# The Mamba output product in high and low float32r parts, with the low parts made by GpSimd and multiplied a step later

## The reference

```python
y = ys + x * D                                   # state output and skip
y = y.reshape(b, L, D_INNER) * silu(z)           # gate, D_INNER = 512
y = y * rsqrt(mean(y * y, axis=-1) + 1e-05) * norm_w
return y @ out_w.T                               # 512 -> 256
# later: concatenate([v, h]) @ fc_w.T + fc_b     # folded into out_w by the kernel
```

## Time and profile before

| | us |
|---|---|
| median of 3 runs | 2471.05 |
| lowest, highest | 2468.98, 2473.85 |
| the profiled execution | 2475.43 |
| its span | 2473.6 |

### The profile page before, as it was taken

How to read it: one execution, slowest core, us unless ns; L and a number is a source line. 1 busy time by engine, 2 the same in 40 slices (tenths; PEclk the granted TensorE clock), 3 DMA queues, 4 the chain that set the end, 5 groups by cost and what they waited for, 6 DMA issues and landing times. The chain is left out here.

```text
span 2473.6 us, 42475 instructions
## 1 busy us (share of the span) xinstructions
PE 2144.9 (87%) x16632; PEld 1392.3 (56%) x16632; DVE 2005.4 (81%) x2384; ACT 1297.6 (52%) x2834; POOL 1015.1 (41%) x513
## 2 busy tenths in 40 slices
PE   8999967787787776666999978999999999999998
PEld 7877512231242221114777747777777777777776
DVE  4426799998989999994877757888888888888886
ACT  3337667767857764541232335555555555555552
POOL 1103789988989999980110001111111111111111
PEclk9999989998999999997999989999999999999999
DMA  7769332223121221103332224232222323333332
GB/s 236 247 193 260 92 70 36 42 51 75 20 53 19 37 42 23 20 12 97 109 96 77 77 65 79 76 78 72 69 69 73 78 76 95 93 88 86 86 78 60
DMA packets 299431, 204.44 MB, mean 83 GB/s; under 512 B 201696, under 2 KB 279008, under 8 KB 294624
## 3 DMA queue, kind: packets, MB, share of 16 engines
q1 hardware_dynamic: 286816, 151.39, 25.2%
q0 software_dynamic: 8704, 33.56, 3.7%
q10 hardware_dynamic: 3712, 16.78, 2.8%
HBM read 133.76 MB, written 67.90 MB: 82 GB/s over the span
## 5 line engine op out<-in xcount | busy, mean ns | idle before, releaser
L285 DVE TENSOR_TENSOR att_av<-att_att,att_v2ps 128x2816 f32<-128x2816 f32 (+2 forms) x288 | 776.0, 2752 | 37.8 <-PE att_bank L464 34.9
L285 POOL TENSOR_TENSOR att_av<-att_att,att_v2sb 128x1280 f32<-128x1280 f32 x256 | 744.8, 2931 | 54.4 <-PE att_bank L464 49.6
L464 PE MATMUL att_bank<-att_av,att_w 128*32 128x512 f32 x4096 | 551.8, 623 | 221.0 <-DVE att_av L285 191.8
L464 PEld LDWEIGHTS att_bank<-att_av,att_w 128*32 128x32 f32 x4096 | 135.1, 111 | 576.3 <-issue 283.9
L1681 DVE SCALAR_TENSOR_TENSOR mb_cv<-mb_bank,mb_cw,mb_cv 128x504 f32<-128x504 f32 (+2 forms) x480 | 343.2, 731 | 126.5 <-ACT mb_cv L1504 121.6
L630 ACT ACTIVATE att_ev<-att_bank 128x512 f32<-128x512 f32 x512 | 297.5, 595 | 272.0 <-PE att_bank L464 225.9
L1324 POOL TENSOR_TENSOR mb_rstd<-mb_ms,mb_neghalf 128x4 f32<-128x4 f32 x32 | 32.2, 1008 | 795.6 <-DVE mb_ms L1725 795.6
L1385 PE MATMUL mb_bank<-mb_xT_hi,dt_win_hi 128*128 128x512 f32 x576 | 242.0, 420 | 36.8 <-DVE mb_cv L1681 35.4
L1443 PE MATMUL mb_bank<-mb_wf,mb_y 128*128 128x256 f32 x1024 | 247.0, 389 | 0.9 <-DVE mb_y L1721 0.9
L1385 PE MATMUL mb_bank<-mb_xT_lo,dt_win_hi 128*128 128x512 f32 x576 | 229.2, 398 | 0.0
L1385 PE MATMUL mb_bank<-mb_xT_hi,dt_win_lo 128*128 128x512 f32 x576 | 229.1, 398 | 0.0
(11 more groups left out here) (182 smaller groups left out, 3328.3 us busy)
## 6 DMA issues: line engine op xcount, KB each, us to landing
att_xin<-in_x SPq DMA_DIRECT2D x32, 512.0 KB, 4.5
qk_t<-att_qk POOLq DMA_DIRECT2D x16, 1024.0 KB, 5.0
v<-att_vs POOLq DMA_DIRECT2D x16, 1024.0 KB, 5.5
mixed_t<-att_ev SPq DMA_DIRECT2D x1024, 8.0 KB
mb_dAb<-dA_rows SPq DMA_DIRECT2D x32, 512.0 KB, 5.9
mb_dAb<-dA_cols SPq DMA_DIRECT2D x32, 512.0 KB, 5.7
att_q<-qk_t ACTq DMA_DIRECT2D x8, 1024.0 KB, 10.8
att_kb<-qk_t ACTq DMA_DIRECT2D x64, 128.0 KB, 8.4
```

The costliest lines, as they stand in the source:

```text
L285: return eng.tensor_tensor(av[t % 2][:, :, d0:d1, :], a.unsqueeze(2).broadcast_to((P, 2, d1 - d0, N)), v2.unsqueeze(1).broadcast_to((P, 2, ...
L464: mm = pe.matmul(bank[r % NB][s * M:(s + 1) * M, :], w[i // WB % 2][:, i % WB, s, :], av[r // 2 % 2][:, i % 2, s * STRIP_D:(s + 1) * STRIP ...
```

## The change

The output product is split as the input projection is. `y` is rounded to a float32r part `y_["hi"]`, and `y_["lo"]` is what is left; `wf` becomes a pair as well. GpSimd makes both parts of y. The products with y's high part stand where `project` stood; those with its low part run a step later, between the fourth and the fifth group of the next input projection. Each output tile now has a bank of its own (`O_[t]`). `scale_out` moves behind nine of the fifteen taps, `times_g` ahead of it. The buffer `pv` is gone: the earlier result is loaded into the output buffer `ot` and added in place.

```diff
--- before.py
+++ after.py
@@ -1126,6 +1126,7 @@
         PR_ = bank[0:3]
         G_ = bank[3]
         YA_, YB_ = bank[4:6], bank[6:8]
+        O_ = bank[4:8]
         PAIR = SEQS // 2
         NT = TOK // P
         GR = CT + 1
@@ -1138,12 +1139,11 @@
         neghalf = sb("neghalf", [P, TT])
         win_hi, win_lo = carried.win_hi, carried.win_lo
         raw, dtt, step_of_dt, dtb, nega = carried.raw, carried.dt, carried.step, carried.dtb, carried.nega
-        wf = [sb(f"wf{d}", [P, CT, E]) for d in range(2)]
+        wf = [{n: sb(f"wf{d}_{n}", [P, CT, E], F32R) for n in ("hi", "lo")} for d in range(2)]
         cw, cb = [[sb(f"{n}{d}", shape) for d in range(2)] for n, shape in (("cw", [P, GR, TAPS]), ("cb", [P, GR]))]
         dskip, normw = [[sb(f"{n}{d}", [P, CT]) for d in range(2)] for n in ("dskip", "normw")]
         bias = sb("bias", [P, E])
         xin = [sb(f"xin{u}", [P, TT, E]) for u in range(2)]
-        pv = [sb(f"pv{u}", [P, TT, E]) for u in range(2)]
         ot = [sb(f"ot{u}", [P, TT, E]) for u in range(2)]
         xT_hi, xT_lo = sb("xT_hi", [P, KT, CHUNK], F32R), sb("xT_lo", [P, KT, CHUNK], F32R)
         cv = sb("cv", [P, GR, CHUNK])
@@ -1154,6 +1154,7 @@
         dAb = sb("dAb", [P, PAIR, NH * L])
         inj = sb("inj", [P, PAIR, NH, L])
         S = sb("S", [P, PAIR, NH * L])
+        y_ = {n: sb(f"y_{n}", [P, CT, CHUNK], F32R) for n in ("hi", "lo")}
         y = sb("y", [P, CT, CHUNK])
         ssr = sb("ssr", [P, CHUNK])
         ms, rstd = sb("ms", [P, TT]), sb("rstd", [P, TT])
@@ -1182,6 +1183,7 @@
         xtok_done, xtok_copied, g_done = sem("xtok_done"), sem("xtok_copied"), sem("g_done")
         inj_ready, scanned, s_ready = sem("inj_ready"), sem("scanned"), sem("s_ready")
         y_done, y_read, gated, squared = sem("y_done"), sem("y_read"), sem("gated"), sem("squared")
+        wf_hi_ready, y_hi_ready, y_lo_ready = sem("wf_hi_ready"), sem("y_hi_ready"), sem("y_lo_ready")
         ss_done, ss_copied, col_done, col_read, rstd_ready = (sem("ss_done"), sem("ss_copied"), sem("col_done"),
                                                               sem("col_read"), sem("rstd_ready"))
         out_done, out_read = sem("out_done"), sem("out_read")
@@ -1236,8 +1238,8 @@
                     if c == NCHUNK:
                         for u in range(2):
                             sp.wait_ge(o_stored[u], NCHUNK // 2 * 16)
-                    sp.wait_ge(out_read, TT * (c - 1))
-                    move("p", c, pv[c % 2], False, pv_loaded[c % 2])
+                    sp.wait_ge(o_stored[c % 2], io_value(c - 2))
+                    move("p", c, ot[c % 2], False, pv_loaded[c % 2])
 
             def load_decay(c):
                 if c < ALL:
@@ -1323,13 +1325,29 @@
                 need(pool, out_read, TT * c)
                 pool.tensor_tensor(rstd[:, :], ms[:, :], neghalf[:, :], ALU.pow).then_inc(rstd_ready, 1)
 
+            def y_hi(c, half):
+                need(pool, out_done, TT * c)
+                pool.wait_ge(gated, 2 * c + half + 1)
+                s = slice(2 * half, 2 * half + 2)
+                pool.tensor_copy(y_["hi"][:, s, :], y[:, s, :]).then_inc(y_hi_ready, 1)
+
+            def y_lo(c, half):
+                pool.wait_ge(y_hi_ready, 2 * c + half + 1)
+                s = slice(2 * half, 2 * half + 2)
+                pool.tensor_tensor(y_["lo"][:, s, :], y[:, s, :], y_["hi"][:, s, :], ALU.subtract).then_inc(y_lo_ready, 1)
+
             inject(0)
             pool.wait_ge(scanned, PAIR)
             inject(1)
             for k in range(ALL):
+                y_hi(k, 0)
+                y_hi(k, 1)
+                if k + 1 < ALL:
+                    pool.wait_ge(scanned, PAIR * (k + 2))
+                y_lo(k, 0)
+                y_lo(k, 1)
                 root(k)
                 if k + 2 < ALL:
-                    pool.wait_ge(scanned, PAIR * (k + 2))
                     inject(k + 2)
 
         @block.tensor
@@ -1434,15 +1452,23 @@
                                                    start=True, stop=True)
                         mm.then_inc(y_done, 1)
 
-            def project(c, t):
-                for m in range(CT):
-                    if t == 0 and m == 0:
-                        pe.wait_ge(y_read, 4 * c + 2)
-                    if t == 0 and m % 2 == 0:
-                        pe.wait_ge(gated, 2 * c + m // 2 + 1)
-                    mm = pe.matmul(YA_[t // 2][:, (t % 2) * E:(t % 2 + 1) * E], y[:, m, t * P:(t + 1) * P],
-                                   wf[way(c)][:, m, :], start=(m == 0), stop=(m == CT - 1))
-                if t % 2:
+            def project_hi(c, half, tiles):
+
+                pe.wait_ge(y_hi_ready, 2 * c + half + 1)
+                for t in tiles:
+                    if half == 0 and t % 2 == 0:
+                        pe.wait_ge(y_read, 4 * c + t + 2)
+                    for m in (2 * half, 2 * half + 1):
+                        for wn in ("hi", "lo"):
+                            pe.matmul(O_[t][:, 0:E], y_["hi"][:, m, t * P:(t + 1) * P], wf[way(c)][wn][:, m, :],
+                                      start=(m == 0 and wn == "hi"), stop=False)
+
+            def project_lo(c):
+                pe.wait_ge(y_lo_ready, 2 * c + 2)
+                for t in range(TT):
+                    for m in range(CT):
+                        mm = pe.matmul(O_[t][:, 0:E], y_["lo"][:, m, t * P:(t + 1) * P], wf[way(c)]["hi"][:, m, :],
+                                       start=False, stop=(m == CT - 1))
                     mm.then_inc(out_done, 1)
 
             def sum_squares(c):
@@ -1467,6 +1493,10 @@
                 if k >= 0 and k + 1 < ALL:
                     for i in range(NG):
                         group(k + 1, i)
+                        if i == 3 and k > 0:
+                            project_lo(k - 1)
+                if k == ALL - 1:
+                    project_lo(k - 1)
                 if k >= 0:
                     y_products(k)
                 for n, (_, _, _, first) in enumerate(PARTS):
@@ -1483,12 +1513,12 @@
                 if k == -1:
                     fold(1)
                 if k >= 0:
-                    project(k, 0)
-                    project(k, 1)
+                    project_hi(k, 0, range(TT))
+                    project_hi(k, 1, range(TT // 2))
                     sum_squares(k)
-                    project(k, 2)
+                    project_hi(k, 1, range(TT // 2, TT))
                     columns(k)
-                    project(k, 3)
+            project_lo(ALL - 1)
 
         @block.scalar
         def _(act):
@@ -1616,8 +1646,13 @@
             def scale_by_norm(d):
                 dve.wait_ge(folded, d + 1)
                 for m in range(CT):
-                    dve.tensor_scalar(wf[d][:, m, :], (YA_, YB_)[d][m // 2][:, (m % 2) * E:(m % 2 + 1) * E],
-                                      normw[d][:, m:m + 1], None, ALU.mult).then_inc(wf_ready, 1)
+                    dve.tensor_scalar(wf[d]["hi"][:, m, :], (YA_, YB_)[d][m // 2][:, (m % 2) * E:(m % 2 + 1) * E],
+                                      normw[d][:, m:m + 1], None, ALU.mult).then_inc(wf_hi_ready, 1)
+                for m in range(CT):
+                    dve.wait_ge(wf_hi_ready, CT * d + m + 1)
+                    dve.scalar_tensor_tensor(out=wf[d]["lo"][:, m, :], in0=(YA_, YB_)[d][m // 2][:, (m % 2) * E:(m % 2 + 1) * E],
+                                             scalar=normw[d][:, m:m + 1], in1=wf[d]["hi"][:, m, :],
+                                             op0=ALU.mult, op1=ALU.subtract).then_inc(wf_ready, 1)
 
             def zero_first_part():
                 for q in range(2):
@@ -1700,7 +1735,7 @@
 
             def add_skip(c, half):
                 if half == 0:
-                    need(dve, out_done, 2 * c)
+                    need(dve, y_lo_ready, 2 * c)
                     need(dve, squared, 2 * c)
                 for q in range(2):
                     dve.wait_ge(y_done, 4 * c + 2 * half + q + 1)
@@ -1731,9 +1766,9 @@
                     dve.wait_ge(rstd_ready, c + 1)
                     if c >= 2:
                         dve.wait_ge(o_stored[c % 2], io_value(c - 2))
-                dve.wait_ge(out_done, 2 * c + t // 2 + 1)
-                dve.scalar_tensor_tensor(out=ot[c % 2][:, t, :], in0=YA_[t // 2][:, (t % 2) * E:(t % 2 + 1) * E],
-                                         scalar=rstd[:, t:t + 1], in1=pv[c % 2][:, t, :] if way(c) else bias[:, :],
+                dve.wait_ge(out_done, TT * c + t + 1)
+                dve.scalar_tensor_tensor(out=ot[c % 2][:, t, :], in0=O_[t][:, 0:E],
+                                         scalar=rstd[:, t:t + 1], in1=ot[c % 2][:, t, :] if way(c) else bias[:, :],
                                          op0=ALU.mult, op1=ALU.add).then_inc(out_read, 1)
 
             zero_first_part()
@@ -1758,19 +1793,14 @@
                         for j, back in which:
                             tap(c, j, back)
 
-                taps((0, 1))
```

(16 more changed lines are left out.)

## The result

| | before | after |
|---|---|---|
| median of 4 runs, us | 2472.26 | 2453.22 |
| lowest, highest | 2468.98, 2473.85 | 2450.41, 2455.41 |
| the profiled execution | 2475.43 | 2450.41 |
| its span | 2473.6 | 2448.2 |

What follows compares the result with a forecast made beforehand. PE was taken as the bound, DVE having 3.8 us of slack in a step. 30 intervals x 1.7 = 51 us saved, less 9 around the steps, gives 42: 2471.05 - 42 = 2429 us, range 2405 to 2475.

Steps and rivals of the forecast that it cites:

- the plain step: Last stage, a step without dt work: falls from 29.89 to 28.2 us, 1.7 shorter.
- both loops: PE's work and waits, 28.2 us; and scans, low parts, low products, four groups, seed, taps, gate, scans, also 28.2.
- C: Rival, output product: short matmuls cost 0.162 us each, 2474 us in all, no change; chance 0.09.
- D: Rival, output product: weight load not hidden behind 256 columns, 0.207 us per matmul, 2540 us in all; chance 0.14.
- The price from which on the gain was to be gone: Output product: from 0.155 us per short float32r matmul, the 51 us saved shrink to the 9 lost.
- B: Rival, GpSimd's subtractions: low parts take 2.9 us each instead of 2.38, step 29.2, 2459 us in all; chance 0.16.
- the weights' scaling: Around the steps: eight more instructions scale the low output weights, four ahead of the first scans, costing 2 us.
- the end: Last step: nothing covers the low parts, and at the very end they lie beside the high products; 4 us together.
- The cast: GpSimd's rounding of y to its high part: 1.6 us for 1024 elements, the second done at 24.2, before PE asks.
- the taps' order: DVE's taps, three of the first group together: PE waits 0.2 us instead of 0.8 ahead of the fourth group.
- step (2) under "Around the steps": First twelve steps: the dt work, 5.6 us over twelve steps, loses DVE's slack, costing 3 more.
- Rival A: GpSimd's second cast holds up DVE's first scan, 0.4 us a step, step 28.6, 2441 us in all; chance 0.18.

Runs made afterwards that it cites:

- e9: The kernel before with only the changed kernel's VectorE order of taps, `times_g` and `scale_out`: 2466.82 us, ratio 0.9988 to before.
- e1: The changed kernel with the softplus pieces of dt ahead of the scans of their step on VectorE: 2435.65 us, ratio 0.9872 to before.
- e4: The changed kernel with the softplus's second instruction, a subtraction, cut to 8 columns, other columns uncorrected: 2450.54 us in a single run.
- e7: The changed kernel with each GpSimd subtraction cut in two of 512 elements, four in a step: 2448.45 us, ratio 0.9926 to before.
- e5: The changed kernel without GpSimd's subtractions, the low products reading y's high part instead: 2416.82 us, ratio 0.9798 to before.
- e3: The changed kernel with e1's edit and the low products behind the fifth projection group instead of the fourth: 2424.28 us, ratio 0.9813 to before.
- e8: e3 with `mean_square` ahead of the last scan instead of behind it: 2418.34 us, ratio 0.9787 to before.

## Why the prediction was right and wrong

**Right: the plain step.** 28.2 forecast, 28.30 measured, with both loops side by side as described. 48 matmuls cost 6.3 (24 between 2014.65 and 2017.70, eight in 1.07, sixteen in 2.16) against 6.24. Their distance is 0.12, under the 0.130 taken; what makes up for it is 0.1 to 0.2 at each change of kind. C (0.162) and D (0.207) are out. (The price from which on the gain was to be gone, 0.155, is 0.159 by the forecast's own sum: 27.8 + 48 x 0.029 + 0.4 = 29.6, 0.3 less a step, 9 in 30.) The Trainium skill, "TensorE: Matmul & The Clock Gate", part 3, "The mechanism", has a line by which a weight load overlaps matmuls in flight only if the row group differs; a sentence ahead of it also names the background weight buffer as a target for which a load is pulled ahead. The trace doesn't agree with the line: each of these matmuls has a 128x128 load of its own (PE and PEld both count 17144 in the profile's head), all on the same rows, and they start 0.12 apart.

**Right in size:** the subtraction 2.38 (B is out), the weights' scaling, 1.1 for 2, and the end: 2.3 in the last interval and 0.7 in the one ahead of it, for 4. In that step PE waits 5.08 for the low parts, where the forecast had 4.8 of GpSimd, partly overlapped. The cast was mis-sized, 1.04 for 1.6, on the safe side: it is what kept it off the scan.

**Right in sum, wrong in its parts: the taps' order.** The forecast counted 0.6 of the 1.7 us for the smaller wait ahead of the fourth group. e9 gives 0 for that alone. By my reading two loops of nearly equal length were closed before as well, one over PE and one over DVE from tap to gate, and the gain needed both shortened. The sum, made by walking through the new step, had it right.

**Wrong: step (2) under "Around the steps", the dt work.** It was put at 5.6 + 3, on the ground that DVE loses slack. It is 370.0 - 12 x 28.3 = 30.4, so 21.8 more than forecast, nearly the whole miss of 23. I had walked through a plain step only, and moved GpSimd's subtractions to behind the scans, "free". But in five of the twelve steps DVE's dt instructions stand right there. e1 takes them away from GpSimd and gets 18.2 back; e4 and e7 show what the wait is made of. Of the other 3.6, most is not from that wait: in e5, with no subtraction, the dt work still costs 346.2 - 12 x 27.94 = 10.9, 2.3 over the 8.6. DVE has no slack for it, and this part of the reasoning was sound, only small by 2.

**Rival A had the mechanism and the wrong place.** It asked who has two SBUF inputs beside the cast, found the scan, and priced it at 0.4 a step. The scan was missed by 0.03 us. The question wasn't asked for the subtractions. Asked with the order of the code at hand, it would have found seven dt instructions at 2 us each: 2429 + 14 = 2443, still 10 under what came. Nor is it right that no run showed the wait yet. The trace of before has it once, ahead of step 0, where a DVE instruction of the dt work with two inputs in SBUF meets `inject`:

```profile
1514.60 1.15 DVE L1636 SCALAR_TENSOR_TENSOR dt_dt_e<-dt_dt_x 128x256 f32<-128x256 f32 x1
```

```profile
1514.33 4.32 POOL L1317 TENSOR_TENSOR mb_inj<-mb_diag,dt_dt 128x512 f32<-128x512 f32 x4 [33.93 <-DVE mb_S L1690]
```

It takes 1.15, and 0.42 in e1, where it stands ahead of the scans. And rival A does come in one step of after, the last but one, which has no split: there the scans follow the gate at once and meet the cast. The two scans take 3.12 instead of 2.33, the cast 1.84 instead of 1.04, and PE waits 1.24 for it.

```profile
2411.29 3.12 DVE L1725 TENSOR_TENSOR_SCAN mb_S<-mb_dAb,mb_inj 128x512 f32<-128x512 f32 x2
```

```profile
2411.50 1.84 POOL L1332 CAST mb_y_hi<-mb_y 128x1024 fp32r<-128x1024 f32 x1 [1.79 <-DVE mb_y L1756]
```

What stays open: why the twelve steps of e1 and e3 still take 11.6 and 17.3 more than twelve of their plain ones, when before needed 5.6 more and e8 needs 7.8. e8 shows that the wait for `mean_square` is part of it; the rest isn't assigned. Nor was after run with the old order of taps: there `scale_out` would stand ahead of taps on which the low products depend, and the engines would wait for each other for ever.

## What to carry to other kernels

When work moves to GpSimd, list every DVE instruction with two SBUF inputs that can meet it, in every kind of step, not only in the plain one. Each is priced at the rest of one GpSimd instruction, however small it is itself, and a chain of them at one each. It is cheap to put the few that meet it elsewhere (18 us in twelve steps here), and a wait that PE feels often hangs on the small instruction queued behind them. A wait that an edit shortens is a gain only if the loop of the other engine shortens as well.

## What the runs showed that was not expected

- A DVE subtraction of 128x8 took 2.19 us beside a GpSimd one of 2.38; 128x256 undisturbed takes 0.43.
- The wait goes both ways: two GpSimd subtractions took 5.64 beside scans, 4.77 without them, and a cast 1.84 instead of 1.04.
- DVE instructions with one of their inputs in PSUM were not slowed by it: four taps 2.92 beside the subtraction.
- Float32r matmuls with 256 columns follow each other every 0.12 us at a granted clock of 1.00, the upper level (2.4 GHz). In the last step they do so behind 1.99 us of idle, and then the clock falls in the middle of them, to 0.50, and they stand 0.21 apart. The low products of that step, behind 5.08 of idle, run at 0.50 from the start and take 3.79 instead of 2.16. The timeline of PE, and the busy time of stretches with the granted clock as the figure behind POOL:

```profile
2422.61 3.79 PE L1470 MATMUL mb_bank<-mb_wf_hi,mb_y_lo 128*128 128x256 f32 x16 [5.08 <-POOL mb_y_lo L1337]
...
2434.18 0.41 PE L1463 MATMUL mb_bank<-mb_wf_hi,mb_y_hi 128*128 128x256 f32 x1
2434.39 0.41 PE L1463 MATMUL mb_bank<-mb_wf_lo,mb_y_hi 128*128 128x256 f32 x1
```

```profile
2422.60:2426.40 3.80, 3.79 (x16) 3.49 (x16) 1.45 (x3) 0.00 (x0) 0.92 (x1) 0.50 0.00 0
...
2432.50:2433.80 1.30, 1.30 (x11) 1.30 (x12) 1.27 (x2) 0.00 (x0) 0.00 (x0) 1.00 0.63 195
2434.00:2437.00 3.00, 2.91 (x14) 2.62 (x13) 0.10 (x1) 1.06 (x1) 2.77 (x2) 0.50 0.16 49
```
